# Gated linear attention stage of a decoder kernel: projections of four batches per weight tile, scores in row groups

## The reference

```python
def _L2_attn_ref(x, norm_w, Wq, Wk, Wv, Wbeta, bbeta, Wig, big, Wog, bog, Wout, bout):
    h = x * jax.lax.rsqrt(jnp.mean(x * x, axis=-1, keepdims=True) + 1e-06) * norm_w
    q, k, v = (heads(Wq), heads(Wk), heads(Wv))
    q = _apply_rope(q, cos, sin)
    k = _apply_rope(k, cos, sin)
    beta, ig, og = (gate(Wbeta, bbeta), gate(Wig, big), gate(Wog, bog))   # sigmoids, one per token and head
    def step(M, inp):
        q_t, k_t, v_t, f_t, g_t, o_t = inp
        M = M * f_t[..., None, None] + g_t[..., None, None] * scale * (k_t[..., :, None] * v_t[..., None, :])
        y_t = jnp.einsum('bhd,bhde->bhe', q_t, M) * o_t[..., None]
        return (M, y_t)
    ...
    return jnp.einsum('bld,ed->ble', y, Wout) + bout
```

## Time and profile before

| | |
|---|---|
| median of 3 runs | 2669.88 us (2664.28 to 2676.25) |
| profiled execution, its own time | 2671.13 us |
| its span | 2669.3 us |
| granted TensorE clock, mean | 0.903 |
| PE / PEld busy | 2273.0 us (85%) / 1805.9 us (68%) |
| DVE / ACT / POOL busy | 1499.4 (56%) / 1146.9 (43%) / 476.3 us (18%) |

### The profile page before, as it was taken

The page is one execution under the profiler, slowest core; times in us unless marked ns, Lnnn a source line. Parts: engine busy times, 40 slices in busy tenths (PEclk is TensorE's granted clock), DMA queues, the critical chain, the costliest instruction groups (busy, mean ns, idle before and its releaser), DMA issues. The chain is left out here.

```text
span 2669.3 us, 43007 instructions
## 1 busy us (share of the span) xinstructions
PE 2273.0 (85%) x15178; PEld 1805.9 (68%) x15178; DVE 1499.4 (56%) x3444; ACT 1146.9 (43%) x3103; POOL 476.3 (18%) x697
## 2 busy tenths in 40 slices
PE   6799664659999976869987969899987999799997
PEld 3566432227777754559876638789975665699997
DVE  3566658995444443555555544456554555555565
ACT  4566344543334333533211534433422565455553
POOL 0200018982000010100033420000013222100001
PEclk8899788899999986669988979989988999799999
DMA  3000012210000004324210024222210000233331
GB/s 108 9 2 2 32 65 76 73 51 32 1 1 1 1 30 129 103 83 151 92 41 5 1 60 120 80 94 93 91 43 9 6 8 1 85 107 106 104 111 61
DMA packets 46180, 151.38 MB, mean 57 GB/s; under 512 B 16967, under 2 KB 19115, under 8 KB 43960
## 3 DMA queue, kind: packets, MB, share of 16 engines
q1 hardware_dynamic: 46012, 149.21, 17.3%
HBM read 137.70 MB, written 11.50 MB: 56 GB/s over the span
## 5 line engine op out<-in xcount | busy, mean ns | idle before, releaser
L2433 PE MATMUL ps<-l1a_zc,tables_sb 128*128 128x400 f32 x256 | 108.8, 558 | 95.2 <-POOL l1a_zc L2362 60.3
L2433 PEld LDWEIGHTS ps<-l1a_zc,tables_sb 128*128 128x128 f32 x256 | 47.3, 202 | 156.7 <-POOL l1a_zc L2362 88.3
L1930 ACT ACTIVATE l1x_probs<-ps,l1x_nmax 100x361 f32<-100x361 f32 x128 | 70.8, 558 | 189.2 <-DVE l1x_nmax L2012 189.2
L2373 POOL TENSOR_TENSOR l1a_dbx<-l1a_dx,l1a_rows 128x400 f32<-128x400 f32 x128 | 130.1, 1049 | 6.9 <-DMA l1a_rows<-l1a_rows_spilled 4.8
L2781 DVE TENSOR_TENSOR l3f_act_out<-l3f_act_out,l3f_gates 128x800 f32<-128x800 f32 x80 | 79.4, 992 | 82.1 <-ACT l3f_act_out L2737 82.1
L2785 DVE TENSOR_TENSOR l3f_hg_low<-l3f_act_out,l3f_hg_high 128x800 fp32r<-128x800 f32 x80 | 79.4, 993 | 62.9 <-ACT l3f_hg_high L2743 62.9
L2737 ACT ACTIVATE l3f_act_out<-ps,l3f_biases 128x800 f32<-128x800 f32 x80 | 74.4, 930 | 91.9 <-PE ps L2626 91.9
L2625 PE MATMUL ps<-l3f_x_high,l3f_w_high 128*128 128x400 f32 x320 | 111.4, 348 | 0.0
L2386 ACT ACTIVATE ps<-l1a_delta,weights 128x400 f32<-128x400 f32 x128 | 76.5, 598 | 81.1 <-DVE ps L2416 53.1
L2624 PE MATMUL ps<-l3f_x_high,l3f_w_low 128*128 128x400 f32 x320 | 110.9, 346 | 0.5 <-DVE l3f_w_low L2715 0.5
L2626 PE MATMUL ps<-l3f_x_low,l3f_w_high 128*128 128x400 f32 x320 | 110.8, 346 | 0.0
(11 more groups left out here) (665 smaller groups left out, 6446.5 us busy)
## 6 DMA issues: line engine op xcount, KB each, us to landing
l3f_landing<-l_ffn_units SPq DMA_DIRECT2D x40, 513.0 KB, 3.5
l3f_gates<-l3f_gates SPq DMA_DIRECT2D x40, 400.0 KB, 3.3
l2x_a_taps<-l2x_taps_spread SPq DMA_DIRECT2D x8, 1912.5 KB
l2f_landing<-l_ffn_units SPq DMA_DIRECT2D x17, 771.0 KB, 4.2
l1a_rows<-l1a_rows_spilled SPq DMA_DIRECT2D x32, 400.0 KB, 3.4
l1f_gates<-l1f_gates SPq DMA_DIRECT2D x16, 800.0 KB, 4.0
l1f_positions<-l1f_staged SPq DMA_DIRECT2D x16, 621.9 KB
l1f_landing<-l_ffn_units SPq DMA_DIRECT2D x16, 512.0 KB, 3.2
```

The source lines that it names most:

```text
L2373: pool.tensor_tensor(dbx[:, n % BUFS, :], dx[:, j, m, :], rows[:, g % RING, 0, :], ALU.mult).then_inc(s.dbx_ready, 1)
L2433: pe.matmul(y_bank(m), st.ident, zc[:, n % DONE, :], start=(i == 0), stop=(i == NS - 1)).then_inc(s.sum_done, 1)
```

## The change

- `qk` and `rqk` are laid out by tile first, then batch. The products of queries and keys are made tile by tile (i) with the tokens of all four batches moving, 400 columns (bank 2i+1), all plain ones ahead of all swapped ones (bank 2i), after the value products of all four batches.
- ScalarE's copy and VectorE's rotation thus go by tile i instead of by batch j; the waits keep their form.
- `q_pad`, its mask in the weight pack (4 of its columns) and its semaphore are gone. The scores of four heads are four products over 32 partitions each, in four row groups, to four banks; a pair of batches shares these banks and one semaphore step.
- The product of scores and decay goes by pairs of batches and row group r, so it reads every fourth head of two batches; the heads wait for all four of a pair.

```diff
--- before.py
+++ after.py
@@ -3082,7 +3082,7 @@
     wvg, wout = view("a6vg"), view("a6o")
     VG = D + 3 * H
     norm_w, gate_bias = st.w["a6norm"][0:S, :], st.w["a6bgates"][0:S, :]
-    cos, sin, head_mask = st.w["a6cos"], st.w["a6sin"], st.w["a6heads"]
+    cos, sin = st.w["a6cos"], st.w["a6sin"]
     js = range(TURN)
     with ExitStack() as ctx:
         def sb(n, shape):
@@ -3090,8 +3090,7 @@
 
         ss, ms = sb("ss", [S, TURN]), sb("ms", [S, TURN])
         hT = sb("hT", [P, TURN, KT, S])
-        qk, rqk = sb("qk", [P, TURN, 2 * KT, S]), sb("rqk", [P, TURN, 2 * KT, S])
-        q_pad = sb("q_pad", [P, TURN, H, S])
+        qk, rqk = sb("qk", [P, 2 * KT, TURN, S]), sb("rqk", [P, 2 * KT, TURN, S])
         vg = sb("vg", [S, TURN, VG])
         beta_pad = sb("beta_pad", [P, TURN, S])
         entries, decay = sb("entries", [S, TURN, H, S]), sb("decay", [S, TURN, H, S])
@@ -3102,7 +3101,7 @@
                 pool.memset(beta_pad[:], 0.0).then_inc(s.first_zero, 1)
 
         sems = ["sq_ready", "ms_ready", "rms_ready", "h_ready", "h_turned", "hT_ready", "vg_ready", "qk_ready", "rqk_ready",
-                "vg_done", "gates_done", "qk_done", "rope_step", "rotated", "q_spread", "beta_turned", "beta_done", "f_ready",
+                "vg_done", "gates_done", "qk_done", "rope_step", "rotated", "beta_turned", "beta_done", "f_ready",
                 "entries_ready", "decay_ready", "scores_ready", "weighed_ready", "heads_done", "o_ready", "o_turned", "oT_ready"]
         with nc.Fori(0, B // TURN) as turn, stage_sems(nc, sems + NORM_SEMS, looped=True) as s, nc.Block() as block:
             x_b = lambda j: st.X[:, turn * TURN + j, :]
@@ -3121,10 +3120,6 @@
 
                     pool.tensor_tensor(entries[:, j], st.ident[0:S, 0:S].unsqueeze(1).to_broadcast([S, H, S]),
                                        vg[:, j, D:D + H].unsqueeze(2).to_broadcast([S, H, S]), ALU.mult).then_inc(s.entries_ready, 1)
-                    pool.wait_ge(s.rotated, j + 1)
-                    for m in range(KT):
-                        pool.tensor_tensor(q_pad[:, j, m * HPT:(m + 1) * HPT, :], wide(qk[:, j, m, :], HPT),
-                                           head_mask.unsqueeze(2).to_broadcast([P, HPT, S]), ALU.mult).then_inc(s.q_spread, 1)
                 for j in js:
                     rstd_pool(pool, st, s, j)
                 for j in js:
@@ -3142,20 +3137,15 @@
                     for k in range(KT):
                         last = pe.matmul(st.ps[0:S, 2 * j, 0:VG], hT[:, j, k, :], wvg[:, k, :], start=(k == 0), stop=(k == KT - 1))
                     last.then_inc(s.vg_ready, 1)
+                for turned in range(2):
                     for i in range(2 * KT):
-                        w, m = (wq, wk)[i // KT], i % KT
+                        w, m = ((wq, wk), (wrq, wrk))[turned][i // KT], i % KT
+                        if turned:
+                            pe.wait_ge(s.vg_done, 2 * (i + 1))
                         for k in range(KT):
-                            last = pe.matmul(st.ps[:, 2 * j + 1, i * S:(i + 1) * S], w[:, k, m * P:(m + 1) * P], hT[:, j, k, :],
+                            last = pe.matmul(st.ps[:, 2 * i + 1 - turned, 0:TURN * S], w[:, k, m * P:(m + 1) * P], hT[:, :, k, :],
                                              start=(k == 0), stop=(k == KT - 1))
-                    last.then_inc(s.qk_ready, 1)
-                for j in js:
-                    pe.wait_ge(s.vg_done, 2 * (j + 1))
-                    for i in range(2 * KT):
-                        w, m = (wrq, wrk)[i // KT], i % KT
-                        for k in range(KT):
-                            last = pe.matmul(st.ps[:, 2 * j, i * S:(i + 1) * S], w[:, k, m * P:(m + 1) * P], hT[:, j, k, :],
-                                             start=(k == 0), stop=(k == KT - 1))
-                    last.then_inc(s.rqk_ready, 1)
+                        last.then_inc((s.qk_ready, s.rqk_ready)[turned], 1)
                 for j in js:
                     pe.wait_ge(s.gates_done, j + 1)
                     pe.wait_ge(s.qk_done, j + 1)
@@ -3167,15 +3157,19 @@
                         last = pe.matmul(st.ps[0:S, 2 * j + h // 4, (h % 4) * S:(h % 4 + 1) * S],
                                          st.ident[:, h:h + 1].to_broadcast([P, S]), beta_pad[:, j, :], start=True, stop=True)
                     last.then_inc(s.f_ready, 1)
-                for j in js:
-                    pe.wait_ge(s.decay_ready, 2 * (j + 1))
-                    pe.wait_ge(s.q_spread, KT * (j + 1))
-                    for h in range(H):
-                        last = pe.matmul(st.ps[0:S, 2 * j + h // 4, (h % 4) * S:(h % 4 + 1) * S], qk[:, j, KT + h // HPT, :], q_pad[:, j, h, :],
-                                         start=True, stop=True)
+                pe.wait_ge(s.rotated, 2 * KT)
+                for first in range(0, TURN, 2):
+                    pe.wait_ge(s.decay_ready, 2 * (first + 2))
+                    for j in range(first, first + 2):
+                        for m in range(KT):
+                            at = (KT * (j - first) + m) * S
+                            for r in range(HPT):
+                                group = slice(HD * r, HD * (r + 1))
+                                last = pe.matmul(st.ps[0:S, 2 * first + r, at:at + S], qk[group, KT + m, j, :], qk[group, m, j, :], start=True, stop=True,
+                                                 tile_position=(HD * r, 0))
                     last.then_inc(s.scores_ready, 1)
                 for j in js:
-                    pe.wait_ge(s.weighed_ready, 2 * (j + 1))
+                    pe.wait_ge(s.weighed_ready, HPT * (j // 2 + 1))
                     for h in range(H):
                         last = pe.matmul(st.ps[0:S, 2 * j, h * HD:(h + 1) * HD], decay[:, j, h, :], vg[:, j, h * HD:(h + 1) * HD], start=True, stop=True)
                     last.then_inc(s.heads_done, 1)
@@ -3199,7 +3193,7 @@
                     act.activation(hT[:, j], tiles(2 * j, KT), ACT.Copy).then_inc(s.hT_ready, 1)
                 for j in js:
                     act.wait_ge(s.qk_ready, j + 1)
-                    act.activation(qk[:, j], tiles(2 * j + 1, 2 * KT), ACT.Copy).then_inc(s.qk_done, 1)
+                    act.activation(qk[:, j], tiles(2 * j + 1, TURN), ACT.Copy).then_inc(s.qk_done, 1)
                     act.wait_ge(s.vg_done, 2 * (j + 1))
                     act.activation(vg[:, j, D:VG], vg[:, j, D:VG], ACT.Sigmoid).then_inc(s.gates_done, 1)
                 for j in js:
@@ -3224,9 +3218,9 @@
                     dve.tensor_tensor(vg[:, j, D:VG], st.ps[0:S, 2 * j, D:VG], gate_bias, ALU.add).then_inc(s.vg_done, 1)
                 for j in js:
                     dve.wait_ge(s.rqk_ready, j + 1)
-                    dve.tensor_tensor(rqk[:, j], tiles(2 * j, 2 * KT), wide(sin, 2 * KT), ALU.mult).then_inc(s.rope_step, 1)
+                    dve.tensor_tensor(rqk[:, j], tiles(2 * j, TURN), wide(sin, TURN), ALU.mult).then_inc(s.rope_step, 1)
                     dve.wait_ge(s.qk_done, j + 1)
-                    dve.tensor_tensor(qk[:, j], qk[:, j], wide(cos, 2 * KT), ALU.mult).then_inc(s.rope_step, 1)
+                    dve.tensor_tensor(qk[:, j], qk[:, j], wide(cos, TURN), ALU.mult).then_inc(s.rope_step, 1)
                     dve.wait_ge(s.rope_step, 2 * (j + 1))
                     dve.tensor_tensor(qk[:, j], qk[:, j], rqk[:, j], ALU.add).then_inc(s.rotated, 1)
                 for j in js:
@@ -3235,12 +3229,12 @@
                     for i in range(2):
                         dve.tensor_tensor_scan(decay[:, j, 4 * i:4 * i + 4, :].rearrange("s h t -> s (h t)"), st.ps[0:S, 2 * j + i, 0:4 * S],
                                                entries[:, j, 4 * i:4 * i + 4, :].rearrange("s h t -> s (h t)"), 0.0, ALU.mult, ALU.add).then_inc(s.decay_ready, 1)
-                for j in js:
-                    dve.wait_ge(s.decay_ready, 2 * (j + 1))
-                    dve.wait_ge(s.scores_ready, j + 1)
-                    for i in range(2):
-                        part = decay[:, j, 4 * i:4 * i + 4, :]
-                        dve.scalar_tensor_tensor(part, st.ps[0:S, 2 * j + i, 0:4 * S].rearrange("s (h t) -> s h t", h=4), float(HD) ** -0.5, part,
+                for first in range(0, TURN, 2):
+                    dve.wait_ge(s.decay_ready, 2 * (first + 2))
+                    dve.wait_ge(s.scores_ready, first // 2 + 1)
+                    for r in range(HPT):
+                        part = decay[:, first:first + 2].rearrange("s j (m r) t -> s j m r t", r=HPT)[:, :, :, r, :]
+                        dve.scalar_tensor_tensor(part, st.ps[0:S, 2 * first + r, 0:4 * S].rearrange("s (j m t) -> s j m t", j=2, m=KT), float(HD) ** -0.5, part,
                                                  ALU.mult, ALU.mult).then_inc(s.weighed_ready, 1)
                 for j in js:
                     dve.wait_ge(s.heads_done, j + 1)
@@ -3708,8 +3702,7 @@
```

(4 more changed lines are left out.)

## The result

| | before | after |
|---|---|---|
| median of 22 runs each | 2669.06 us (2660.03 to 2676.25) | 2662.84 us (2656.66 to 2669.87) |
| ratio after to before | | 0.998, 95% interval 0.9971 to 0.9989 |
| span of the profiled execution | 2669.3 us | 2656.8 us |
| granted clock, mean | 0.903 | 0.901 |

The change brings 0.2%, some 5 us (3 to 8 by the interval). The gain is clear of zero, and it is less than the 0.5% that the prediction asked of a faster kernel. The spans of the two profiled executions differ by 12.5 us, but one execution scatters by 13 to 16 us with either kernel, so I measure the stage itself: from the first value product of a turn (L3143 before, L3138 after) to that of the next, and from the second turn's to the first L3328 product of the next stage (L3322 after).

What follows compares the result with a forecast made beforehand. In the changed stage, VectorE was taken to hold the stretch before the scans, though TensorE leads the whole program. Terms -12.0 + 1.2 + 8.4 = -2.4 us gave a forecast of 2668 us, range 2655 to 2676.

Steps and rivals of the forecast that it cites:

- the most likely case: Earlier scans, then half clock through the head products of both turns: 2668 us, own range 2664 to 2671, chance 0.60.
- rival 1: Clock holds through head products: 2660, or 2656 if full throughout; mixture, one turn each, about 2663 us; chance 0.22.
- earlier scans: Gain from shorter projections and faster rotation before the scans: 6.0 us per turn, 12.0 in all.
- later start of the heads: First head products wait for four weighing instructions instead of two: loss 0.6 us per turn, 1.2 in all.
- clock: TensorE at half clock for all head products, 10.8 us each turn, transposes and output products also slower: loss 8.4 us.
- Projections: TensorE's value products take 5.65 us; query, key and twin products 10.7 us instead of 14.6.
- Rotation: VectorE's rotation without GpSimd's padded queries: first ends near 15.3 us, last at 20.3, gaining 6.0 us per turn.
- Scores: TensorE's scores for a pair of batches, in four row groups: 32 records in 0.96 us.
- Weighing: Product of scores and decay: eight instructions at 0.49 us; heads start 2.1 us after the scans instead of 1.5.
- Output products: Products after the heads: second turn goes from 4.96 to the first turn's 5.56 us, norms passing on about 0.2.
- Rival 2: Low clock does not come back within the output products: 6.8 us per turn, total 2672 us, chance 0.13.
- Rival 3: GpSimd's entries come late and keep all rotations slow, costing 4 to 6 us per turn: 2670 to 2676, chance 0.05.

Runs made afterwards that it cites:

- e2: Changed kernel, with GpSimd again writing two unused tiles of 128 x 400 behind each rotation: 2672.52 us, ratio 1.0017 to the kernel before.
- e3: Changed kernel plus unused TensorE products, 13 behind the first pair's scores and 4 behind the second's: 2661.95 us, ratio 0.9978 to the kernel before.
- e6: e4 with its gate-spreading products moved behind decay products, plus the fillers of e3 and 5 behind the second batch's heads: 2649.50 us.
- e4: Changed kernel with head products turned round in four column groups, output gate applied to the transposed result: 2648.44 us, ratio 0.9925 to the kernel before.

## Why the prediction was right

The time, 2662.8 us, lies in the range of 2655 to 2676, and the trace shows the mechanism of the most likely case: earlier scans, then half clock through all head products. The number was less good than the mechanism. The median is 5 us under the 2668 forecast, below that case's own range (2664 to 2671), and by the time alone the mixture under rival 1 (2663) would have fitted better; it is the granted clock that rules this out. The forecast gain of 2.4 us was half of what the stage shows:

| | earlier scans | later start of the heads | clock | sum |
|---|---|---|---|---|
| forecast | -12.0 | +1.2 | +8.4 | -2.4 us |
| measured, both turns | -13.8 | +0.8 | +8.4 | -4.6 us |

The measured clock term is 2.8 and 5.1 us in the head products, and 0.3 in the transposes and 0.2 behind them in the second turn. Step by step, in the order of the prediction:

- **Projections.** Forecast 5.65 and 10.7 us; the rows have 5.58 and 10.91, each with the tail of the last product (5.41 and 10.75 to the next line's start). Right.
- **Rotation.** Forecast scans at 20.3, gain 6.0 per turn. Measured 19.3 and 19.1, gain 7.0 and 6.8. This is the term that was mis-sized most, by 1.8 us in all: I had put the end of the first rotation near 15.3 us and three more at 1.7 each. The entries ended at 13.6 instead of 14, the first rotation at 14.6, and a rotation takes 1.57 when no step is held. That GpSimd made the old rotations slow was argued then and is shown by e2.
- **Scores.** 0.96 us for 32 records in row groups, as in the other stage. The second pair took 1.10 and 1.28, with the clock falling in it, and ended within the 2.1 us that the weighing needs.
- **Weighing.** 3.91 us for eight, strided or not. The head products start 2.0 us after the weighing begins, forecast 2.1; before it was 1.6, not 1.5, so the loss is 0.4 us per turn where 0.6 was put.
- **Clock.** Forecast: half for all head products of both turns, 10.8 us each, loss 2.7 + 5.1. Measured 10.87 and 10.88. The price taken from the 4.8 us at half clock in the earlier trace rows held to 1%. That the light stretch in front makes the clock fall was only argued then; e3 shows it for the early fall, and also that full gaps alone don't keep the clock.
- **Output products.** 5.50 and 5.39 us against 5.56 forecast for both; the clock came back some 3.5 us after they began. Rival 2 needed it later than 5.
- **Rival 1**, the clock holds, did not come. Of the kernels with the change it held through the head products only in e6, with the gaps filled and the head products in column groups.
- **Rival 3**, late entries, did not come: one step held, for 0.7 us.

By turn, the first gained 3.8 us (2.7 forecast) and the second 0.8 (-0.3 forecast). Of these 1.1 us more in each, the rotation accounts for 1.0 and 0.8, and the smaller delay of the head products for 0.2.

What remains open: how far the 12.5 us between the two profiled spans, beyond the stage's 4.6, belong to the change. By the interval of the 22 runs of each, 3 to 8 us, most of the rest does not; 3.6 us of it lie in front of the stage. How few fillers would hold the clock in e6 without delaying the weighing was not tried.

## What to carry to other kernels

Time saved in front can be paid back by TensorE's clock: here 13.8 us of earlier scans became 4.6, and 8.4 of the 9.2 us lost came from the lower clock, because the lighter stretch in front of a long series of products dropped them to half clock. Before counting such a gain, look at what the products behind it take at either clock. If each loads 100 columns of weights to move 32, turn the product round and use column groups: e4, which also drops eight transposes and four copies per turn, was worth three times the whole change. And take from GpSimd whatever lies beside VectorE's steps with two SBUF inputs, even if nobody waits for it.

## What was not expected of the hardware

- The head products' time follows the weight loads: for loads of 100 columns a record takes 0.09 us at granted clock 1.00 whether 32 columns move (64 in 5.76) or 100 (64 decay products in 5.89), and 0.114 for loads of 128. It follows the clock too: 0.17 us at 0.50 for the 32 columns.
- In a series of head products in which TensorE shows no idle time the clock fell about 2.1 and 2.7 us after their start (e3) and 3.0 us (first turn), but in the second turn before the change only behind them, 6.0 us after their start. In column groups, with fillers around them, it did not fall (e6).
- A series of 32 records in column groups takes 1.56 us at half clock and 0.89 at full. For all 64 that is 3.5 times as fast at half clock, and 3.2 times at full, as the head products in their old form.
